# First attention: four score banks and single banks for the maxima

## What is computed

```python
attn = jnp.einsum('bhqd,bhkd->bhqk', q, k) * SCALE          # 4 batches, 16 heads, D = 16, 1024 x 1024
alibi = diff[None, :, :] * slopes[:, None, None] * MAX_BIAS  # diff = min(key - query, 0)
attn = attn + alibi[None]
w = jax.nn.softmax(attn, axis=-1)
out = jnp.einsum('bhqk,bhkd->bhqd', w, v)
```

## Time and profile before

| | |
|---|---|
| median of 3 runs | 1915.79 us (1911.1 to 1917.71) |
| profiled execution | 1916.35 us |
| its span | 1914.6 us |
| PE busy | 1654.9 us (86%) |
| DVE busy | 1296.4 us (68%) |
| ACT busy | 992.3 us (52%) |
| self-attention, maxima of the first group to its last instruction | 118.9 to 927.9 us |

### The profile page before, as it was taken

One profiled execution on the slowest core, in us unless ns is written; L12 is line 12 of the kernel. 1 busy time (PEld: TensorE's weight loads), 2 busy tenths in 40 slices (PEclk: granted clock), 3 DMA queues, 4 the chain that ended last, 5 costly groups with the idle time before them and its releaser, 6 DMA issues. The chain is left out here.

```text
span 1914.6 us, 36288 instructions
## 1 busy us (share of the span) xinstructions
PE 1654.9 (86%) x14824; PEld 1080.1 (56%) x14824; DVE 1296.4 (68%) x2288; ACT 992.3 (52%) x1692; POOL 404.2 (21%) x268
## 2 busy tenths in 40 slices
PE   7858999999999999998584799877993999999970
PEld 7734444444444444443374555545762888988870
DVE  6687888888888888883294446752333777777736
ACT  5324777777777777777342166853442333333310
POOL 6440000000000000000223100000453344444430
PEclk9957999999999999999797567977996999999995
DMA  7877444444444444400546766313213233334225
GB/s 254 218 186 210 63 68 65 66 66 68 67 66 65 69 63 68 64 14 8 182 143 179 111 94 112 80 45 133 90 41 113 67 92 92 92 92 92 37 31 178
DMA packets 131409, 183.93 MB, mean 96 GB/s; under 512 B 30904, under 2 KB 95560, under 8 KB 130188
## 3 DMA queue, kind: packets, MB, share of 16 engines
q1 hardware_dynamic: 117804, 159.56, 39.4%
q0 software_dynamic: 13440, 22.07, 5.5%
HBM read 114.95 MB, written 69.99 MB: 97 GB/s over the span
## 5 line engine op out<-in xcount | busy, mean ns | idle before, releaser
L638 DVE TENSOR_REDUCE att_row_max<-att_ring 128x2 f32<-128x1024 f32 x512 | 602.4, 1220 | 108.0 <-PE att_ring L704 56.9
L622 ACT ACTIVATE att_w_exp<-att_s_ps 128x512 f32<-128x512 f32 x1024 | 547.8, 596 | 231.9 <-PE att_s_ps L747 156.4
L774 PE MATMUL att_a_ps<-att_w_exp,att_v_group 128*32 128x512 f32 x2048 | 273.6, 606 | 0.2 <-ACT att_w_exp L622 0.2
L733 PE MATMUL att_s_ps<-att_q_stack,att_k_stack 62*128 62x512 f32 x640 | 181.5, 480 | 0.0
L733 PEld LDWEIGHTS att_s_ps<-att_q_stack,att_k_stack 62*128 62x128 f32 x640 | 84.3, 184 | 123.9 <-ACT att_w_exp L622 112.8
L2156 ACT ACTIVATE ex_hid<-ex_h_ps,ex_b 128x512 f32<-128x512 f32 x128 | 87.2, 686 | 116.4 <-DVE ex_h_lo L2211 66.6
L2112 POOL DMA_INDIRECT x_scr<-ex_y,ex_home x64 | 106.7, 1666 | 181.4 <-DVE ex_y L2201 166.8
L560 POOL COPY att_eyes<-keep_slope_eye 128x384 bf16<-128x384 bf16 x16 | 8.1, 507 | 641.1 <-PE att_s_ps L747 631.8
L2211 DVE TENSOR_TENSOR ex_h_lo<-ex_hid,ex_h_hi 128x512 fp32r<-128x512 f32 x128 | 138.8, 1085 | 4.4
L704 PE MATMUL att_ring<-att_k_stack,att_q_stack 60*128 60x512 f32 x640 | 131.4, 451 | 6.3 <-DVE att_att L665 3.2
L747 PE MATMUL att_s_ps<-att_eyes,keep_past_bf 64*128 64x64 bf16 x3840 | 133.4, 193 | 0.0
(11 more groups left out here) (296 smaller groups left out, 3544.0 us busy)
## 6 DMA issues: line engine op xcount, KB each, us to landing
first_w_raw<-ew SPq DMA_DIRECT2D x16, 1024.0 KB
att_k_stack<-qk_scr SPq DMA_DIRECT2D x120, 128.0 KB
cr_q_stack<-q_scr SPq DMA_DIRECT2D x48, 256.0 KB, 9.3
keep_k_stack<-qk_scr SPq DMA_DIRECT2D x72, 128.0 KB
rows_scr<-att_zeros POOLq DMA_DIRECT2D x8, 1040.0 KB, 22.0
ex_rows<-rows_scr SPq DMA_DIRECT2D x16, 520.0 KB
att_q_stack<-qk_scr SPq DMA_DIRECT2D x60, 128.0 KB
qk_scr<-qkv_t_hi SPq DMA_DIRECT2D x7, 1024.0 KB, 4.3
```

The costliest lines, as they stand in the source:

```text
L622: nc.scalar.activation(w_exp[(STEPS * g.n + st) % SETS][h][:, :], s_ps[v % BANKS][:, :], ACT.Exp).then_inc(exp_done, 1)
L638: nc.vector.tensor_reduce(out, ring[place.slot][:, :, :], AX.X, ALU.max).then_inc(ring_free, 1)
L733: ins = nc.tensor.matmul(s_ps[v % BANKS][:, :], ks[g.buf][rows, c, j, kt * P:(kt + 1) * P], qs[g.buf][rows, j, c * CH:(c + 1) * CH], start ...
L774: ins = nc.tensor.matmul(a_ps[32 * h:32 * h + 32, :], vg[g.buf][:, kt, h * VW:h * VW + 32], w_exp[(STEPS * g.n + st) % SETS][h][:, :], sta ...
```

## The change

`BANKS` is 4, and `RING_SLOTS` is 3 with single banks. Each head's maxima tile of a unit has a place of its own in the ring, with its own wait, its own signal and its own reduction of 512 columns; one reduction took 1,024 before. The order of a step on PE is now: four scores, the first unit of maxima, the values, the transposes where there are any, the second unit. Before it was: two scores, values, transposes, two scores, two units. DVE's order follows: transposes' readers now stand between the reductions of the two units.

```diff
-BANKS = 3
+BANKS = 4
-RING_SLOTS = 2
+RING_SLOTS = 3
 def ring_order(first, with_max):
     order = []
     for st in range(STEPS):
+        order += [("max", 2 * st, i) for i in range(2) if with_max]
         if st == 1:
             order.append(("top", 1))
...
-        order += [("max", 2 * st + i) for i in range(2) if with_max]
+        order += [("max", 2 * st + 1, i) for i in range(2) if with_max]
...
-        ring = [s.pb(f"ring{i}", (P, 2, 512)) for i in range(RING_SLOTS)]
+        ring = [s.pb(f"ring{i}") for i in range(RING_SLOTS)]
...
-            def maxima(u, place):
-                dve.wait_ge(ring_full, place.at + 1)
+            def maxima(n, u):
                 half, j, q, kk = max_unit(u)
-                out = row_max[half][:, :, :].rearrange("p (h q) k -> p h q k", q=4)[:, 2 * j:2 * j + 2, q, kk]
-                nc.vector.tensor_reduce(out, ring[place.slot][:, :, :], AX.X, ALU.max).then_inc(ring_free, 1)
+                for i in range(2):
+                    place = PLACES[n, "max", u, i]
+                    dve.wait_ge(ring_full, place.at + 1)
+                    out = row_max[half][:, :, :].rearrange("p (h q) k -> p h q k", q=4)[:, 2 * j + i, q, kk:kk + 1]
+                    nc.vector.tensor_reduce(out, ring[place.slot][:, :], AX.X, ALU.max).then_inc(ring_free, 1)
...
             def max_main(g, u, i, place):
+                pe.wait_ge(ring_free, place.at + 1)
...
-            def max_pair(g, u, place):
+            def max_pair(g, u, window):
                 half, j, q, kk = max_unit(u)
-                pe.wait_ge(ring_free, place.at + 1)
-                for i in range(2):
-                    ins = max_main(g, u, i, place)
+                places = [PLACES[window, "max", u, i] for i in range(2)]
+                ins = [max_main(g, u, i, places[i]) for i in range(2)]
                 if kk == half:
                     last = 3 if q == 3 else 1
                     for n in range(last + 1):
-                        for i in range(2):
-                            ins = max_bias(g, u, i, place, n, last)
-                ins.then_inc(ring_full, 1)
+                        ins = [max_bias(g, u, i, places[i], n, last) for i in range(2)]
+                for i in range(2):
+                    ins[i].then_inc(ring_full, 1)
...
                     score_pair(g, st, 0)
+                    score_pair(g, st, 2)
+                    if with_max:
+                        max_pair(n, 2 * st, g.n)
                     if st > 1:
                         values(g, st - 2)
...
-                    score_pair(g, st, 2)
                     if with_max:
-                        for i in range(2):
-                            max_pair(n, 2 * st + i, PLACES[g.n, "max", 2 * st + i])
+                        max_pair(n, 2 * st + 1, g.n)
```

More of the change, by code:

```diff
@@ L442, in ring_places @@
 def ring_places():
-    order = [(None, "max", u) for u in range(TOP0_AT + 1)] + [(None, "top", 0)]
-    order += [(None, "max", u) for u in range(TOP0_AT + 1, UNITS)]
+    order = [(None, "max", u, i) for u in range(TOP0_AT + 1) for i in range(2)] + [(None, "top", 0)]
+    order += [(None, "max", u, i) for u in range(TOP0_AT + 1, UNITS) for i in range(2)]
     for n in range(NG):
-        order += [(n, what, i) for what, i in ring_order(n == 0, n < NG - 1)]
+        order += [(n, *what) for what in ring_order(n == 0, n < NG - 1)]
     order.append((NG - 1, "acc", "end"))
@@ L654, in copy_top @@
                 dve.wait_ge(top_out[half], 16 * g.n + 16)
-                nc.vector.tensor_copy(neg_top_t[half][:, :], ring[place.slot][0:32, 0, 0:P]).then_inc(ring_free, 1)
+                nc.vector.tensor_copy(neg_top_t[half][:, :], ring[place.slot][0:32, 0:P]).then_inc(ring_free, 1)
             def normalise(g, c, place):
@@ L659, in normalise @@
                 dve.wait_ge(ring_free, place.at + RING_SLOTS)
-                sums = ring[place.slot][:, 0, :].rearrange("p (q h e) -> p q h e", q=4, h=HG)
+                sums = ring[place.slot][:, :].rearrange("p (q h e) -> p q h e", q=4, h=HG)
                 nc.vector.reciprocal(recip[:, :, :], sums[:, :, :, D]).then_inc(recip_done, 1)
@@ L669, in _ @@
             for u in range(UNITS):
-                place = PLACES[None, "max", u]
-                maxima(u, place)
+                maxima(None, u)
                 if u % 16 == 15:
-                    top_parts(g0, u // 16, place)
+                    top_parts(g0, u // 16, PLACES[None, "max", u, 1])
                 if u == TOP0_AT:
@@ L678, in window @@
                 for st in range(STEPS):
+                    if with_max:
+                        maxima(g.n, 2 * st)
                     if st == 1:
@@ L686, in window @@
                         normalise(g, 0, PLACES[g.n, "acc", 0])
-                    for i in range(2):
-                        if with_max:
-                            maxima(2 * st + i, PLACES[g.n, "max", 2 * st + i])
+                    if with_max:
+                        maxima(g.n, 2 * st + 1)
                     if with_max and st % 8 == 7:
-                        top_parts(g.plus(1), st // 8, PLACES[g.n, "max", 2 * st + 1])
+                        top_parts(g.plus(1), st // 8, PLACES[g.n, "max", 2 * st + 1, 1])
             windows(window)
@@ L701, in max_main @@
             def max_main(g, u, i, place):
+                pe.wait_ge(ring_free, place.at + 1)
                 half, j, q, kk = max_unit(u)
                 rows, tok = slice(64 * i, 64 * i + ROW_TOP), half * CH + q * P
-                return nc.tensor.matmul(ring[place.slot][:, i, :], qs[g.buf][rows, j, tok:tok + P],
+                return nc.tensor.matmul(ring[place.slot][:, :], qs[g.buf][rows, j, tok:tok + P],
                                         ks[g.buf][rows, half, j, kk * CH:(kk + 1) * CH], start=True, stop=kk != half)
@@ L781, in transpose_acc @@
                 for q in range(4):
-                    ins = nc.tensor.transpose(ring[place.slot][:, 0, q * P:(q + 1) * P], acc_sb[c][:, q * P:(q + 1) * P], ident[:, :])
+                    ins = nc.tensor.transpose(ring[place.slot][:, q * P:(q + 1) * P], acc_sb[c][:, q * P:(q + 1) * P], ident[:, :])
                 ins.then_inc(ring_full, 1)
```

8 lines of the change are left out of this document (4 added, 4 removed).

## The result

| | before | changed |
|---|---|---|
| median | 1916.13 us (4 runs) | 1935.10 us (4 runs, 1931.95 to 1939.57) |
| profiled execution | 1916.35 us | 1936.25 us |
| ratio | | 1.0102, 95% interval 1.0078 to 1.0125 |

The account below looks back on a forecast made before the run. The prediction took ACT's answer to PE, not DVE's or PE's own work, as the bound. 1916.35 + 9 (15 windows) + 7 (prologue) - 8 (last window) = 1924 us, range 1904 to 1944.

Parts of the forecast that it names:

- What bounds the kernel before: Attention steps: a closed loop of PE and ACT's exponentials, 2.61 us a plain step, 2.99 with biases.
- Bias steps: Full windows: with the fourth score bank, steps with biases take 2.79 to 2.81 us on PE, against 2.99.
- The new wait in the ring: Plain steps 3 to 8: PE waits 0.28 us for a bank still being reduced; steps go from 2.61 to 2.68.
- +0.43 to values: In the ring's 2.68 us loop: from PE going on with the held maxima tile to values, 0.43 us.
- The accumulator steps: Steps 2 and 10: transposes stand between values and the second maxima pair; 3.76 us for each.
- The 1.60: Steps 2 and 10: normalising lets DVE begin a reduction 1.60 us after the accumulator transposes start.
- Values later, the copy's wait: Steps 1 and 9: ACT's accumulator copy waits for later values; 3.90 and 3.52 us, about 1.15 a window.
- Prologue: Before the windows: DVE waits 0.45 us at each of 16 bias units; net +7 us, bounds +1 and +10.
- Last window: Without maxima, steps go to 2.03 us from 2.60, with biases 2.23 from 2.99; less two copy waits, -8 us.
- that DVE's operations don't overlap: Rival: DVE becomes the bound, four reductions take 2.76 us a plain step; 1938 us, chance 0.12.
- That the ring's and the copy's waits would be absorbed: Faster rival: without ACT's copy wait 1907 us, without the ring's wait too 1862; chance 0.25 in all.
- the inner band, 1921 to 1934: Whole kernel: the forecast's own case, 1921 to 1934 us, likeliest 1924, chance 0.35.

Follow-up runs that it names:

- e8: The changed kernel with three score banks in place of four, the order of a step as changed; 2092.78 us in a single execution.
- e7: The kernel before, but in the last window four score banks (one an unused ring-slot half), four scores in a run and a later copy; 1904.58 us, 0.9921.
- e3: The changed kernel with each maxima reduction over every second of its 512 columns; 1887.71 us, 0.9855 of the kernel before.
- e2: The changed kernel with the joining of the maxima put behind the next step's first unit of reductions; 1934.03 us, 1.0094 of the kernel before.
- e9: The changed kernel with each maxima tile's biases right behind its own matmul, in the prologue only; 1933.03 us, 1.0077 of the kernel before.
- e1: The changed kernel with ACT's accumulator copy behind the fourth exponential of steps 1 and 9, not the second; 1925.16 us, 1.0054 of the kernel before.
- e4: The kernel before with only the maxima split: three score banks, its order of a step, a ring of four single banks; 1918.15 us, 1.0012.
- e10: The changed kernel with the copy later, the joining of the maxima later and the prologue's biases tile by tile; 1914.53 us, 0.9998 of the kernel before.
- e11: The changed kernel with biases behind their own tile in first maxima units of steps 4 to 8, full windows; 1939.23 us, 1.0113 of the kernel before.
- e5: The changed kernel's banks (four for scores, ring of three) with the kernel before's order of a step; 2075.3 us, 1.0820 of the kernel before.

## Why the prediction was right, and where it was off

Point by point, by the intervals of its sum (from the first unit's late tile of one step to that of the next, median over windows 2 to 12; forecast, measured):

| steps | forecast | measured |
|---|---|---|
| 0 | 2.81 | 3.04 |
| 1 (copy) | 3.90 | 3.94 |
| 2 (accumulator) | 3.76 | 3.54 |
| 3 to 7 (plain) | 5 x 2.68 = 13.40 | 2.84 + 3 x 2.78 + 2.84 = 14.02 |
| 8 (plain) | 2.68 | 3.17 |
| 9 (copy) | 3.52 | 3.52 |
| 10 (accumulator) | 3.76 | 3.38 |
| 11, 12, 14, 15 | 4 x 2.81 = 11.24 | 11.44 |
| 13 | 3.21 | 3.17 |
| window | 48.28 | 49.2 |

- *What bounds the kernel before:* right. The waits behind ACT's exponentials went with the fourth bank, and e8 brought them back (175.2 us); in the last window alone, e7 took 10.5 us with it.
- *Bias steps:* right for 12 and 14, 2.82 and 2.83 for 2.79 to 2.81; 11 and 15 took 2.91 and 2.88.
- *The new wait in the ring:* the mechanism is right, and e3 moved it by exactly the 0.27 that was taken from the reduction. **The term "+0.43 to values" was mis-sized.** It came from a tile without biases; behind a late tile with biases it is 0.51, and 0.56 in steps 3 and 7, whose late tiles have twice as many. From the unit's start to the reduction took 0.53 for 0.51. So a plain step is 2.78, not 2.68: with steps 3 and 7, 0.62 a window, 9 us. The 0.02 has the size of the 26 ns that the Trainium skill (TensorE: Matmul & The Clock Gate, The cost: per-tile semaphore tail) gives an increment. The trace speaks against that cause: in steps 12 to 15 the first units signal tile by tile too and are taken at 0.51 to 0.52. What the 0.02 is stays open.
- *What was left out:* the joining of the maxima in front of the first reductions of steps 0 and 8 (+0.23 and +0.49 a window). The forecast named no price for it. e2 shows that it delays the ring, and that moving it helps by 0.22 only. In step 8 0.10 of the 0.49 is not the joining: its second unit carries the biases and is taken at 0.61, which with 0.69, 0.06, 0.43 and 0.99 makes 2.78.
- *The accumulator steps:* forecast too dear by 0.60 together. The 1.60 from the transposes to the next reduction in the earlier trace rows contained DVE's own backlog: the normalising began 0.96 behind the transposes there, right after a reduction, and begins 0.69 behind them in the changed kernel. The 1.60 is then 449.89 - 448.56 = 1.33 (timeline):

```profile
448.56 0.66 PE L787 MATMUL att_ring<-keep_ident,att_acc_sb 128*128 128x128 f32 x4
...
449.89 1.28 DVE L642 TENSOR_REDUCE att_row_max<-att_ring 128x1 f32<-128x512 f32 x2
```

- *Values later, the copy's wait:* right in place and in the length of both steps (3.94 and 3.52 for 3.90 and 3.52). What removing it gives back, 0.72 a window for 1.15, was over-priced, since in step 9 the ring's wait comes next.
- Together the window was missed by 0.94, 14 us over 15: 0.62 + 0.72 - 0.60 and 0.20 of small ones. The first window grew by 2.3, 0.7 more than the others, where the forecast took the same; the 0.7 lies in its first steps, and no run takes it apart.
- *Where a full window's 1.6 comes from:* by the same intervals in the kernel before, steps 3 to 7 cost 0.99 more, the two accumulator steps (2 and 10) 0.99, step 9 0.54, while 11 to 15 gave back 0.68 and 0 and 8 together 0.29.
- *Prologue:* +6.1 for +7, by the mechanism named: 0.37 idle for 0.45 at each bias unit. DVE's part of it grew by 8.5 (46.8 for 38.3), of which the old wait for the transfer took up 2.5. e9 takes the idle time away and leaves 0.60 a reduction.
- *Last window:* -9.1 for -8, by the steps named: the plain ones take 1.96 and 2.11 in turn, 2.03 in the mean. ACT's copy waited there too, 1.8 us of it (e1).
- *The rivals:* that DVE's operations don't overlap is out, they start 0.60 to 0.61 apart and last 0.69, and e4 has twice as many of them at no cost. That the ring's and the copy's waits would be absorbed is out by e1 and e3. The rival of operations that don't overlap named the right engine for the wrong reason: DVE is not busy too long, one reduction is in a chain that is short of a bank. Its 1938 lies nearer to the 1935.10 than the 1924 does, and the inner band, 1921 to 1934, just misses it; that is the mis-sized terms, not that rival. The forecast's reading of the page that it names for this rival is too broad as well: the Trainium skill (VectorE: DVE Perf Modes, The DRAIN you can't avoid) adds in the same paragraph that a next operation that is not held starts earlier, as the 0.60 against 0.69 shows here.

The sum would have been 1916.35 + 6.1 + 2.3 + 22.1 - 9.1 = 1937.8 with the parts as measured, and the profiled execution took 1936.25.

## What to carry to other kernels

A ring's length counts in units of what is written at once: four tiles a step, in pairs, through three banks leaves the second of a pair waiting for a full reduction and what follows on PE for both, although DVE has time to spare. Before banks are moved from one ring to another, write out for each the loop of producer, consumer and what stands between two writes in the queue; the shortest stretch between writes must be longer than ready, reduced and seen together. And give a resource only where its loop binds: the fourth score bank pays 9.1 us in the one window without maxima, 10.5 with the copy moved (e7), and each of the other 15 loses 1.6, of which 0.65 is left when the copy and the joining are moved (e10).

## What the runs showed of the hardware

- A 512-column matmul that PE reaches without a stop is on record for 0.40 us with its bias 0.24 behind; one that starts after a wait for 0.50 with its bias 0.35 behind (e11, clock 1.00). Without biases, values start 0.43 behind a tile that starts after a wait (440.55 to 440.98) and 0.33 behind one that does not (447.24 to 447.56, step 10 of the changed kernel). That a wait costs PE 0.1 us beyond its own length is likely from these pairs, but not shown: 0.42 also stands where nothing waited and the tiles came behind bias matmuls (456.34 to 456.76).
- A reduction of every second column in PSUM lies on the line of the unbroken ones: 256 elements take 419 ns against 685 for 512, 266 less, the 1.04 ns an element of the earlier trace rows. No run here reads 256 neighbouring columns.

```profile
L642 DVE TENSOR_REDUCE att_row_max<-att_ring 128x1 f32<-128x256 f32 x772 | 290.3, 419 | 196.0 <-PE att_ring L717 104.3 <-PE att_ring L709 89.6
```
- Two units of maxima on the same ring of three (e5) and four scores on three banks (e8) take a window to 58.8 and 58.6 us, where the kernel before has 47.6 and the whole change 49.2: neither part can be judged alone.
